# Layer norm of the later groups by tokens along the row, with moments sent through memory, in an attention and expert layer on one core

## What is computed

```
xn = (x - mean(x)) / sqrt(var(x) + 1e-5)             # per token, over its 128 features
h = relu(xn @ nm_w1 + nm_b1);  m = h @ nm_w2 + nm_b2
att = sliding_window_attention(m, ...)               # 32 keys to either side, softmax
gates = sigmoid(xn @ gate_w.T);  the best 8 of 16 experts, weights sum to 2.826
y = sum over the experts of weight * ((silu(xn @ w_gate.T) * (xn @ w_up.T)) @ w_down.T)
y = y + shared expert of the same form, weight 1
out = x + att + y
```

## Time and profile before

| | us |
|---|---|
| median of 3 runs | 722.94 (722.91 to 723.25) |
| the profiled execution | 722.1 |
| its span | 720.2 |
| TensorE with matmuls in flight | 701.5 |
| VectorE busy | 574.2 |
| ScalarE busy | 438.9 |
| GpSimd busy | 399.7 |

### The profile page before, as it was taken

The page is one execution under the profiler, slowest core; times in us unless marked ns, Lnnn a source line. Parts: engine busy times, 40 slices in busy tenths (PEclk is TensorE's granted clock), DMA queues, the critical chain, the costliest instruction groups (busy, mean ns, idle before and its releaser), DMA issues.

```text
span 720.2 us, 10617 instructions
## 1 busy us (share of the span) xinstructions
PE 701.5 (97%) x3384; PEld 577.2 (80%) x3384; DVE 574.2 (80%) x1605; ACT 438.9 (61%) x874; POOL 399.7 (55%) x356
## 2 busy tenths in 40 slices
PE   5889999999999999999999999999999999999997
PEld 4667888888888888888888888888888888888886
DVE  4788788787888878788887888878787887878775
ACT  3575665666656575665766656566655766656573
POOL 3745555546565555565556655555565555655463
PEclk9999999999999999999999999999999999999999
DMA  7704316061250615216061340615215061430600
GB/s 256 256 10 152 130 26 226 29 235 45 90 191 2 234 45 177 103 47 218 16 235 45 109 172 4 236 42 204 76 51 227 4 236 45 130 135 7 244 1 15
DMA packets 36647, 84.72 MB, mean 118 GB/s; under 512 B 7152, under 2 KB 15472, under 8 KB 36592
## 3 DMA queue, kind: packets, MB, share of 16 engines
q1 hardware_dynamic: 36592, 84.05, 33.2%
HBM read 79.32 MB, written 4.72 MB: 117 GB/s over the span
## 4 chain that ended last, share of the span: by engine, by line
PE 93%; DVE 3%; DMA 2%; ACT 1%; issue 0%; POOL 0%; SPq 0%; DVEq 0%
PE ps_y L390 26%; PE ps_u L380 26%; PE ps_g L370 26%; PE bank L348 3%; PE bank L306 3%; PE bank L329 3%; PE bank L318 2%; PE bank L311 2%; PE bank L338 2%; PE ps_y L357 1%; DMA comb_b<-c_dram 1%; DVE ps_u L889 0%; DVE h_lo L895 0%; DVE exp_w_lo L644 0%; DMA xin<-x 0%
## 5 line engine op out<-in xcount | busy, mean ns | idle before, releaser
L969 POOL TENSOR_TENSOR silu_c<-silu,comb_b 128x512 f32<-128x512 f32 x256 | 330.5, 1294 | 300.7 <-ACT silu L564 297.1
L572 ACT ACTIVATE h_hi<-ps_u 128x512 fp32r<-128x512 f32 x272 | 162.5, 598 | 261.7 <-DVE ps_u L889 259.8
L895 DVE TENSOR_TENSOR h_lo<-ps_u,h_hi 128x512 fp32r<-128x512 f32 x272 | 185.7, 683 | 59.9 <-ACT h_hi L572 59.7
L889 DVE TENSOR_TENSOR ps_u<-silu_c,ps_u 128x512 f32<-128x512 f32 x256 | 176.6, 690 | 44.5 <-PE ps_u L380 38.2
L564 ACT ACTIVATE silu<-ps_g 128x512 f32<-128x512 f32 x272 | 161.4, 594 | 0.2
L380 PE MATMUL ps_u<-xn_hi,exp_w_hi 128*128 128x512 f32 x272 | 110.7, 407 | 5.1 <-DVE h_lo L895 5.1
L390 PE MATMUL ps_y<-h_hi,exp_w_hi 128*128 128x512 f32 x272 | 112.7, 414 | 0.4 <-DVE h_lo L895 0.4
L370 PE MATMUL ps_g<-xn_hi,exp_w_hi 128*128 128x512 f32 x272 | 108.3, 398 | 0.0
L370 PE MATMUL ps_g<-xn_lo,exp_w_hi 128*128 128x512 f32 x272 | 108.0, 397 | 0.0
L370 PE MATMUL ps_g<-xn_hi,exp_w_lo 128*128 128x512 f32 x272 | 107.6, 395 | 0.0
L380 PE MATMUL ps_u<-xn_lo,exp_w_hi 128*128 128x512 f32 x272 | 107.5, 395 | 0.0
(11 more groups left out here) (139 smaller groups left out, 982.0 us busy)
## 6 DMA issues: line engine op xcount, KB each, us to landing
comb_b<-c_dram SPq DMA_DIRECT2D x64, 1024.0 KB, 8.7
xin<-x SPq DMA_DIRECT2D x16, 256.0 KB, 3.1
xres<-x_t SPq DMA_DIRECT2D x16, 256.0 KB, 2.7
out_t<-xres SPq DMA_DIRECT2D x16, 256.0 KB, 2.0
exp_raw<-wexp SPq DMA_DIRECT2D x3, 960.0 KB, 9.3
c_dram<-comb_t SPq DMA_DIRECT2D x64, 8.0 KB, 1.8
exp_raw<-wexp SPq DMA_DIRECT2D x1, 384.0 KB, 5.4
att_raw<-watt SPq DMA_DIRECT2D x1, 330.5 KB, 3.4
```

Of the source, the lines that this page charges most:

```text
L572: A(h_t[hbuf(par, s)][0][:], ps_u[(par + s) % 2][:], ACT.Copy).then_inc(s_h_hi, 1)
L889: V.tensor_tensor(ps_u[i][:], src[:], ps_u[i][:], ALU.mult).then_inc(s_h, 1)
L895: V.tensor_tensor(t[1][:], ps_u[(par + s) % 2][:], t[0][:].bitcast(F32), ALU.subtract)\
L969: G.tensor_tensor(silu_c[i][:].rearrange("p (l x) -> p l x", l=2), silu[i][:].rearrange("p (l x) -> p l x", l=2), comb_b[:, :, s1 - 1, :], ...
```

## The change

From group 2 on the tokens are normalised in the layout that the matmuls need, and TensorE turns nothing for them.

- SyncE loads x_t of the group straight into xn in slot 3, once xn_lo of the group before is done, and the token-wise x of one group further. In slot 8 (slot 12 in group 0) it stores the means and inverse deviations of the group two ahead, 2 x 512 numbers, in a small tensor in memory, waits for that, and loads them spread over all partitions into mom_b.
- VectorE no longer normalises. bn_stats moves from slot 12 to slot 0 of the same group (slot 5 in group 0), bn_aggr and the epsilon addition from slot 14 to slot 5 (slot 10 in group 0), and a copy of the four means is added behind them.
- GpSimd takes the power in slot 7 (11 in group 0) instead of 16, subtracts the means in two halves at the end of slots 14 and 15, and multiplies in slot 16.
- ScalarE and VectorE make xn_hi and xn_lo from xn in SBUF, no longer from the PSUM bank.

Groups 0 and 1 are normalised as before.

```diff
+TURNED = 2
+        mom = sb("mom", [P, 2, TILES])
+        mom_b = sb("mom_b", [P, 2, T])
             def load_x(g, par):
-                sp.dma_start(xin[par][:], x[g * T:(g + 1) * T, :].rearrange("(a p) d -> p a d", p=P))\
-                    .then_inc(s_xin[par], 16)
+                rows = x[g * T:(g + 1) * T, :]
+                rows = rows.rearrange("(a p) d -> p a d" if g < TURNED else "(p a) d -> p a d", p=P)
+                sp.dma_start(xin[par][:], rows).then_inc(s_xin[par], 16)
+            def load_turned(g):
+                if g == TURNED:
+                    sp.wait_ge(S["xn_tp"], g)
+                else:
+                    sp.wait_ge(S["xn_lo"], g)
+                sp.dma_start(flat(xn), x_t[:, g * T:(g + 1) * T]).then_inc(s_xt, 16)
+            def spread_moments(g):
+                n = g - TURNED + 1
+                sp.wait_ge(S["rstd"], g + 1)
+                sp.wait_ge(S["mean"], n)
+                sp.dma_start(st_dram.rearrange("k (p a) -> p k a", p=P), mom[:]).then_inc(s_mom_st, 16)
+                sp.wait_ge(s_mom_st, 16 * n)
+                if n > 1:
+                    sp.wait_ge(S["xn"], g)
+                sp.dma_start(mom_b[:], st_dram.rearrange("(o k) t -> o k t", o=1).to_broadcast([P, 2, T]))\
+                    .then_inc(s_mom_b, 16)
...
                     if not last(g, 1):
-                        sp.wait_ge(S["xn"], g + 1)
-                        load_x(g + 2, par)
+                        if first(g):
+                            sp.wait_ge(S["xn"], g + 1)
+                            load_x(g + 2, par)
+                        load_turned(g + 2)
+                    if not last(g, 2):
+                        if first(g):
+                            sp.wait_ge(S["xn"], g + 2)
+                        else:
+                            sp.wait_ge(S["bn"], g + 2)
+                        load_x(g + 3, 1 - par)
+                if s == (12 if first(g) else 8) and not last(g, 1):
+                    spread_moments(g + 2)
...
             def att_early(g, par, s):
-                if s == 1 and more:
+                if s == 1 and g + 1 < TURNED:
                     pe.wait_ge(S["xn"], g + 2)
...
             def xn_hi(g, par):
+                    act.wait_ge(S["xn"], g + 1)
+                A(xn_t[par][0][:], bank[1][:] if g < TURNED else flat(xn), ACT.Copy).then_inc(S["xn_hi"], 1)
...
             def variance(g):
+                if g >= TURNED:
+                    n = g - TURNED
+                    if n > 0:
+                        dve.wait_ge(s_mom_st, 16 * n)
+                    V.tensor_copy(mom[:, 0, :], mv[:, :, 0]).then_inc(S["mean"], 1)
...
-                if s == 0 and more:
-                    normalise(g + 1, 1 - par)
+                if s == 0:
+                    if g + 1 < TURNED:
+                        normalise(g + 1, 1 - par)
+                    elif more2:
+                        moments(g + 2, par)
-                if s == 5 and more:
-                    gate_sum(g + 1)
+                if s == 5:
+                    if more:
+                        gate_sum(g + 1)
+                    if more2 and first(g):
+                        moments(g + 2, par)
+                    elif more2:
+                        variance(g + 2)
...
                     prob_lo(g, 1)
                     if more:
                         route_sum(g + 1)
+                    if first(g):
+                        variance(g + 2)
...
-                if s == 12 and more2:
-                    moments(g + 2, par)
-                if s == 14:
-                    if more2:
-                        variance(g + 2)
-                    if more:
-                        hid_lo(g + 1)
+                if s == 14 and more:
+                    hid_lo(g + 1)
...
             def inverse_std(g):
+                if g > TURNED:
+                    pool.wait_ge(s_mom_st, 16 * (g - TURNED))
+                dst = rstd[:] if g < TURNED else mom[:, 1, :]
+                G.tensor_tensor(dst, var_eps[:], power[:], ALU.pow).then_inc(S["rstd"], 1)
+            def centre(g, half):
+                if half == 0:
+                    pool.wait_ge(s_xt, 16 * n)
+                    pool.wait_ge(s_mom_b, 16 * n)
+                c = slice(half * T // 2, (half + 1) * T // 2)
+                G.tensor_tensor(flat(xn)[:, c], flat(xn)[:, c], mom_b[:, 0, c], ALU.subtract)\
+                    .then_inc(S[f"centred{half}"], 1)
+            def normalise(g):
+                G.tensor_tensor(flat(xn), flat(xn), mom_b[:, 1, :], ALU.mult).then_inc(S["xn"], 1)
...
                 elif not last(g, 1):
+                    normalise(g + 2)
+                if s == (11 if first(g) else 7) and not last(g, 1):
                     inverse_std(g + 2)
+                if s == 14 and not last(g, 1):
+                    centre(g + 2, 0)
+                if s == 15 and not last(g, 1):
+                    centre(g + 2, 1)
```

More of the change, by code:

```diff
@@ L62, in hdist, with layer @@
     return next(d for d in range(1, 2 * STEPS + 1) if order[(p - d) % (2 * STEPS)] == order[p])
-def layer(nc, x, x_t, watt, watt_t, expert_bias, wexp, out_t, c_dram):
+def layer(nc, x, x_t, watt, watt_t, expert_bias, wexp, out_t, c_dram, st_dram):
     ctx = ExitStack()
@@ L154, in layer @@
         s_xres = [sem(f"xres_loaded{i}") for i in range(2)]
+        s_xt = sem("x_t_loaded")
+        s_mom_st = sem("moments_stored")
+        s_mom_b = sem("moments_spread")
         s_const0 = sem("const_cleared")
@@ L189, in layer @@
         s_stored = [sem(f"y_stored{i}") for i in range(2)]
-        names = """bn aggr var_eps rstd xn xn_tp xn_hi xn_lo gate_mm gate_s gate_e
+        names = """bn aggr var_eps rstd mean centred0 centred1 xn xn_tp xn_hi xn_lo gate_mm gate_s gate_e
             gate_1 score select top8 rest weight wsum winv comb comb_t
@@ L522, in xn_hi @@
             def xn_hi(g, par):
-                act.wait_ge(S["xn_tp"], g + 1)
-                A(xn_t[par][0][:], bank[1][:], ACT.Copy).then_inc(S["xn_hi"], 1)
+                if g < TURNED:
+                    act.wait_ge(S["xn_tp"], g + 1)
+                else:
+                    act.wait_ge(S["xn"], g + 1)
+                A(xn_t[par][0][:], bank[1][:] if g < TURNED else flat(xn), ACT.Copy).then_inc(S["xn_hi"], 1)
             def gate_exp(g):
@@ L669, in xn_lo @@
                 dve.wait_ge(S["xn_hi"], g + 1)
-                V.tensor_tensor(xn_t[par][1][:], bank[1][:], xn_t[par][0][:].bitcast(F32), ALU.subtract)\
+                V.tensor_tensor(xn_t[par][1][:], bank[1][:] if g < TURNED else flat(xn), xn_t[par][0][:].bitcast(F32), ALU.subtract)\
                     .then_inc(S["xn_lo"], 1)
@@ L927, in inverse_std @@
                 pool.wait_ge(S["var_eps"], g + 1)
-                G.tensor_tensor(rstd[:], var_eps[:], power[:], ALU.pow).then_inc(S["rstd"], 1)
+                if g > TURNED:
[3 more added lines that the diff above has]
+            def centre(g, half):
+                n = g - TURNED + 1
+                if half == 0:
[5 more added lines that the diff above has]
+            def normalise(g):
+                n = g - TURNED + 1
+                pool.wait_ge(S["centred0"], n)
+                pool.wait_ge(S["centred1"], n)
+                G.tensor_tensor(flat(xn), flat(xn), mom_b[:, 1, :], ALU.mult).then_inc(S["xn"], 1)
             def prologue():
@@ L1010 @@
     c_dram = nc.dram_tensor("c_dram", (2, 2 * E, 2, P), F32, kind="Internal").ap()
-    layer(nc, *args, out_t, c_dram)
+    st_dram = nc.dram_tensor("st_dram", (2, T), F32, kind="Internal").ap()
+    layer(nc, *args, out_t, c_dram, st_dram)
     r = run_bass_kernel_spmd(nc, [arrays], core_ids=[0])
```

## The result

| | before | after |
|---|---|---|
| median of the runs, us | 723.1 (722.91 to 724.0, 4 runs) | 718.27 (717.95 to 718.71, 4 runs) |
| profiled run, us | 722.1 | 717.95 |
| its span, us | 720.2 | 716.2 |
| groups 2 to 14, each | 43.03 | 42.67 |
| group 0, group 1 | 47.18, 43.03 | 47.98, 43.18 |

The ratio is 0.9931 with a 95% interval of 0.9914 to 0.9948, so the kernel is 4.8 us faster, against a forecast of 5.5 (717.4 on the median's scale). A group is counted from its first gate projection to that of the next. The span gives the account: 13 groups at -0.364 on the mean (one of them took 42.70) are -4.73, group 1 +0.15, group 0 +0.80, what lies ahead of group 0 -0.16 and the last group with what follows it -0.12, together -4.06. Forecast were -0.44 in each of 14 groups and +0.6 for group 0.

A forecast was written before the change was run, and what follows sets the result against it. TensorE was taken to bound the steady groups. From the profiled 722.1 us, 6.2 off for the transposes and 0.6 on for group 0 gave 716.5, or 717.4 on the median's scale; range 716.2 to 726.0.

The forecast's parts named there:

- What bounds the kernel: Steady groups: TensorE's issue sets the 43.03 us period; removed work gains its issue time unless another engine becomes late.
- The quartet, 0.44: TensorE, groups 1 to 14: four transposes removed in each, 0.44 us a quartet, 6.2 us in all.
- the 275 ns a transpose: TensorE's transposes at the skill's price: 15.4 us back, ending at 708; chance 1 in 100.
- Who becomes late: VectorE's queue read slot by slot: least spare for TensorE 0.20 us, at h_lo of slot 9; cost 0.
- Slot 5: VectorE: bn_aggr, epsilon addition and copy of means come in, 0.57 us, covered by its waits; cost 0.
- xn_lo behind a product of GpSimd: VectorE, slot 2: xn_lo reading two SBUF tiles is not held up, cost 0; other end about 0.6 us.
- GpSimd: Slots 14 to 16: halves 0.65 to 1.0 us, multiplication 1.3; power of 1.04 in slot 7; cost 0.
- Rival A: Slot 8: GpSimd's power blocks VectorE's second prob_n scaling 0.8 us, 0.6 lost a group, 725.2; chance 0.33 in full.
- TensorE's spare: Slots 8 to 12: TensorE can take 0.20 us of VectorE delay before it waits for h_lo.
- Rivals B and C: B: another engine sets the period, 723.5, chance 0.05; C: moments 3 us late before slot 16, 731, chance 0.03.
- Groups 0 and 1: Variance moved into group 0 and group 1's later comb_b: together +0.6 us, bounds 0 and 1.4.
- the signs that were named: If right: period 42.59, TensorE waits for nothing, transposes 64 + 8 in place of 128, prob_n at most 0.45.

The follow-up runs named there:

- e3: Kernel before without the transposes of groups 2 to 15, nothing else moved (output wrong from group 2): 719.96 us, group 42.82.
- e1: Kernel after with VectorE's xn_lo moved from slot 2 to slot 3, behind the residual addition: 714.57 us, group 42.43.
- e4: Kernel before with the unused tiles mom and mom_b allocated ahead of xn_hi and xn_lo: 719.39 us, group 42.85.
- e10: Kernel before with only the unused tile mom, 32 bytes a partition, ahead of xn_hi and xn_lo: 720.07 us, group 42.85.
- e5: Kernel after with mom and mom_b allocated behind all other tiles: 720.72 us, group 42.82.
- e9: Kernel after with an unused GpSimd multiplication, 128x384, directly ahead of the power in slot 7: 724.75 us, group 43.17.
- e6: Kernel after with an unused GpSimd multiplication, 128x256, directly ahead of the power in slot 7: 719.11 us, group 42.77.
- e8: Kernel after with xn_lo in slot 3 and, in group 0, the moments' spread behind the store of comb: 713.86 us, group 42.43.
- e11: Kernel before with only the unused tile mom_b, 4096 bytes a partition, ahead of xn_hi and xn_lo: 722.77 us, group 43.03.

## Why the prediction was right, point by point

**What bounds the kernel.** Right: TensorE, and work taken from it was worth its issue time "as long as nobody else becomes late". That condition is where the sum broke.

**The quartet, 0.44.** Right. e3 gives 0.21 + 0.23 = 0.44, the part gained and the part lost to the wait; e1 against e4, both with the tiles in the new place, gives 42.85 - 42.43 = 0.42. By the 275 ns a transpose of the Trainium skill, "TensorE: Matmul & The Clock Gate", Part 4, it would have been 1.1 a group: as a cost in the queue that is two and a half times too much here (the page's figure stands beside one for bf16; these transposes are fp32).

**Who becomes late.** The step that failed. I searched VectorE's queue for the h_lo that the up projections wait for, found the smallest spare (0.20, slot 9) and took it for the least of all. The down projections wait for VectorE as well, once a group, and that wait had no spare at all; it stood under no name in the waits because it cost nothing. Slot 2 I looked at for what might delay xn_lo (GpSimd), not for what stands behind xn_lo: h_lo and xres of slot 3. 13 x 0.24 = 3.1 us of the forecast 6.2 went there (e1).

**The place of the tiles.** Not a step of the prediction at all: 0.18 a group in the kernel before (e4, e10), 0.15 in the kernel after (e5), 2.0 to 2.3 us in favour. The two errors are of opposite sign, so that the 717.4 came out within 0.9 of the median (718.27) partly by luck. Without the second the kernel would have been at 720.7, as e5 is, and the forecast off by 3.3, though still within its range.

**Slot 5.** Right. The variance stands between the product and h_lo, in the kernel after, group 6, VectorE:

```profile
300.03 0.17 DVE L704 TENSOR_SCALAR var_eps<-mv 128x4 f32<-128x4 f32 x1
300.11 0.17 DVE L709 COPY mom<-mv 128x4 f32<-128x4 f32 x1
300.18 0.69 DVE L950 TENSOR_TENSOR h_lo<-ps_u,h_hi 128x512 fp32r<-128x512 f32 x1
...
301.58 0.70 DVE L944 TENSOR_TENSOR ps_u<-silu_c,ps_u 128x512 f32<-128x512 f32 x1 [0.23 <-PE ps_u L422]
303.06 0.17 DVE L868 RECIPROCAL row_inv<-row_sum 128x2 f32<-128x2 f32 x1 [0.79 <-ACT prob L598]
```

Against the earlier trace rows the 0.47 ahead of h_lo is used up and the 0.23 and 0.78 behind it stand as they did; with xn_lo out of the way e1 keeps all that the transposes give.

**xn_lo behind a product of GpSimd.** Its records are 684 to 689 ns throughout the kernel after, so the 0 was right and the 0.6 didn't occur.

**GpSimd.** The centring halves took 0.74, the multiplication 1.30 and the power 1.04, all within what the products' rows gave, and nobody waited for them.

```profile
L994 POOL TENSOR_TENSOR xn<-xn,mom_b 128x256 f32<-128x256 f32 x28 | 20.8, 742 | 1.6 <-DMA mom_b<-st_dram 1.6
L1001 POOL TENSOR_TENSOR xn<-xn,mom_b 128x512 f32<-128x512 f32 x14 | 18.2, 1297 | 2.0
L986 POOL TENSOR_TENSOR mom<-var_eps,power 128x4 f32<-128x4 f32 x14 | 14.5, 1037 | 0.0
```

**Rival A.** Its price was about right and its premise wrong. e9 shows what it would have cost (0.51 a group against 0.6, 724.75 against 725.2), the order of the two requests was the unlucky one, and still it didn't come: this power held nothing. That agrees with the argument that I had set against it ("it reads four elements, so it may hold nothing while it computes"), but no run tells whether the operation or the four elements make the difference. TensorE's spare, put at 0.20, was 0.25 to 0.26: the 0.36 of e6 cost 0.10 a group, the 0.76 of e9 0.51. By the rule of the Trainium skill, "SBUF — State Buffer", "Who interferes with whom", the pair is held for the whole instruction: for the products of e6 and e9 the trace agrees to 0.1 us, for the power of 1.03 it doesn't.

**Rivals B and C.** The chain from slot 5 to 12 moved along with TensorE (e1's group is 0.60 shorter than before's), and mom_b landed 3.9 (median) after its issue, so that no steady group waited.

**Groups 0 and 1.** Forecast +0.6 with a bound of 1.4; measured +0.80, and +0.15 in group 1, which is 0.51 over the steady groups: 1.3 in all, at the upper end. Group 1's part is told with e8. In group 0 VectorE does the variance just ahead of an h_lo that it then starts at 56.91, where the kernel before started it at 56.63, having been 0.28 ahead one slot earlier. But no matmul waits from 54 to 70 us in the kernel after, because another thing had made TensorE late. Windows of the kernel after, group 0, after its wait of 2.6 for h_lo:

```profile
50.00:52.00 2.00, 2.00 (x6) 1.56 (x7) 1.96 (x10) 1.50 (x3) 0.32 (x1) 0.58 0.00 0
52.00:54.00 2.00, 2.00 (x10) 1.50 (x8) 2.00 (x7) 0.95 (x2) 0.96 (x1) 0.56 0.00 0
```

The granted clock is 0.58 and 0.56, mostly the 1.2 GHz level, where the kernel before had 1.00 in both. The same windows of e11, whose instructions are those of the kernel before:

```profile
50.00:52.00 2.00, 1.75 (x7) 1.41 (x8) 1.96 (x9) 1.17 (x3) 0.00 (x0) 0.87 0.00 0
52.00:54.00 2.00, 2.00 (x9) 1.61 (x7) 2.00 (x7) 0.90 (x3) 1.29 (x1) 0.50 0.00 0
```

There group 0 took 48.30 against 47.18, so this alone can be worth 1.1, more than the 0.80 in question. All seven profiled kernels that hold the change had it, and of the six without it only e11. The 24 executions of the kernel before that stand beside e9 to e11 divide likewise: 8 with a mean granted clock of 0.999 or 1.000 took 721.66 to 722.33, 16 with less took 722.62 to 724.44, and the profiled one is of the first kind. (Of the four of the kernel after, the one at 1.000 was the slowest, 718.71, so there it isn't seen.) The +0.80 therefore compares a group at full clock with one that was slowed, and how much of it is the variance's is not shown; nor is why the clock falls in one execution and not in another.

**The sum.** Against the profiled run: forecast 716.5, measured 717.95. 14 groups at 0.364 in place of 0.44 make +1.1, group 0 with what group 1 took beyond a steady one, 1.3 in place of 0.6, +0.7, the start and the last group -0.3: +1.5, as measured to the rounding. Of the signs that were named, the transposes are 64 + 8 and prob_n takes at most 0.45; the period is 42.67 and not 42.59, and TensorE's weight loads do wait.

## What to carry to other kernels

Before a bound engine is relieved, list every wait that it makes in one period, also those that cost nothing now, with the time from the release to the instruction that needs it; the smallest of these, and not the smallest of the visible ones, is what the relief is worth until the releasing engine's order is changed too (here one line gave 3.7 us more). A new buffer moves all that are allocated behind it: time the old code with the buffer alone before a gain or a loss is put down to the new instructions. Whether one engine holds up another depended here on the instruction: a product did, a power of the same length on four elements didn't, so a price taken from one kind of instruction has to be tried on the other, by putting each in the same place of the queue.

## What the hardware showed that I had not expected

- With the tiles that TensorE's 128x512 matmuls stream from 32 bytes beside a multiple of 64, a group took 0.18 us more than with them at a multiple of 64 (43.03 against 42.85, in e10 by 32 unused bytes). The Trainium skill, "SBUF — State Buffer", "Operand start alignment", asks only for a multiple of the element size and says that it timed nothing, so the two don't contradict each other.
- A GpSimd power on 128x4 lasted 1.03 us and did not hold up the VectorE scaling that started 0.06 to 0.07 behind it (291 to 294 ns in 13 groups); a GpSimd product of 1.02 us in its place made the scaling 1,053 to 1,058 ns long.
- After TensorE had stood idle for 2.7 us in group 0, the granted clock was 0.87 and 0.50 in the two windows that followed in e11 and 1.00 in the kernel before, which has the same instructions, and e11's group 0 was 1.1 us longer.
